# Edge phase of a graph layer: Q whole in f32, one f32 product per step for the queries, and gathers without waits for products

## The chip, the cores and the metric

The kernel runs on one core of a Trainium2 chip. The metric is the device time of one execution in microseconds. Engines: PE (TensorE, with PEld for its weight loads), DVE (VectorE), ACT (ScalarE), POOL (GpSimd, which here issues indirect DMAs) and SP (SyncE, which issues plain DMAs).

## The reference

One graph layer with attention over edges, then a mixture of experts. Only the first part matters here. N = 3125 nodes, 50000 edges sorted by destination, D = 256 = 4 heads x 64, 64 relations.

```python
enh = node_features + 0.1 * query_emb[None, :]
Q = (enh @ Wq + bq).reshape(N, H, D)
K = (enh @ Wk + bk).reshape(N, H, D)
V = (enh @ Wv + bv).reshape(N, H, D)
rel = rel_w[edge_relations]
mod_k = K[src] + 0.2 * rel[:, None, :]
scores = jnp.einsum('ehd,ehd->eh', Q[dst], mod_k) / D ** 0.5
seg_max = jax.ops.segment_max(scores, dst, num_segments=N)
ex = jnp.exp(scores - seg_max[dst])
denom = jax.ops.segment_sum(ex, dst, num_segments=N)
w = ex / denom[dst]
agg = jax.ops.segment_sum(w[:, :, None] * V[src], dst, num_segments=N)
```

What follows (output projection, layer norm, gate, top 2 of 16 experts) is the same in both kernels.

## The kernel before

**Tiling.** The nodes are 25 tiles of 128. The sorted edges are cut into 440 steps of up to 128 edges; two steps are a pair (220 pairs, numbered p), and all edges of a pair have destinations in one node tile. Four steps are a quad (110, numbered g), eight an octet (55, numbered o), 32 a chunk (14).

**Before the edges (to about 85 us).** The rows of x are normed, turned and multiplied into K and V, which go to a table in HBM (`kv_table`, 2 KB per node). Then Q is projected, tile by tile (`project_q`, L1659): five tiles before the first edges, the others beside pairs 0 to 14 (`q_tiles_at`). Q of each tile is kept as three bf16 pieces whose sum is the f32 value, in `q3`: ACT writes the first (`high_piece`, L1425), DVE the rest of it (`rest_of_q`, L743), ACT the second piece (`middle_piece`, L1429) and DVE the third (`low_piece`, L748).

**The edge phase (about 85 to 880 us).** Each engine has one order of work, written out by hand:

- POOL gathers K and V of the sources, four gathers per quad of 128 rows x 2 KB (`gather`, L626) into `ring`. The gathers of quad g wait until quad g - 4 is reduced (`a_red`), and two of them (u = 1, 2) also for the first and the second product of quad g - 3 (`a_prod`).
- SP loads, per octet, the destinations and types of the edges, spread over all partitions (`d_row`, `t_row`).
- DVE makes the 0/1 masks: `node_hot` (L857) compares the destinations with the partition number and writes `hot_t`, one mask of 128 x 1024 per octet, bf16; `type_hot` (L862) does it for the relations. Then, per octet: `add_relation` to K of two quads (L870), `multiply` by Q[dst] of four pairs (L877), `reduce` two quads to scores (L883), `add_sums` of four pairs, 26 pairs late (L889). Once per chunk come the running maxima (`maxima`, L896), and the factors by which sums are rescaled. `node_hot(o + 2)` is made in octet o between the fourth `multiply` and the second `reduce`.
- PE fetches Q[dst] with products of mask and Q (`queries`, L1724), three pairs ahead of `multiply` (AHEAD = 3), since three banks of PSUM take turns. It also makes the relations' rows (`relations`, L1736), turns the masks (`turn_hot`, L1744: eight transposes of the octet o - 4, in slot 2 of octet o, so behind `queries(4o + 5)` and the sums of that slot), and adds weighted V into per-node sums (`sums`, L1762, f32, 2 products per pair).
- ACT copies the turned masks (`take_hot`, L1492) and weighs V with the softmax weights (`weigh`, L1505).

A semaphore's `wait(eng, n)` lets the engine go on once event n has happened. `hot_t` has HB_N = 7 buffers: `node_hot(m)` waits until `turn_hot(m - HB_N)` is done, through `b_tr`. The mask of a quad is read by `queries`, by `turn_hot` and, one column, by a copy to `first`.

Of the kernel before, what the change touches and what calls it, by code (L numbers as in the profile page):

```python
# [5 lines left out]
F32 = mybir.dt.float32  # L6
BF16 = mybir.dt.bfloat16
# [49 lines left out]
HB_N = 7  # L57
# [87 lines left out]
def build(nc, A, out):  # L145
    ctx = ExitStack()
    with ctx:
# [89 lines left out]
        q3 = sb("q3", [P, NODE_TILES, 3 * D], BF16)  # L237
# [66 lines left out]
        q3_flat = q3[:, :, :].rearrange("p t c -> p (t c)").bitcast(F32)  # L304
        at[0] = 0
        x_again = carve(q3_flat, NT * D)
        xre = x_again.rearrange("p (t c) -> p t c", c=D)
        w_o = carve(q3_flat, KC * D).rearrange("p (k n) -> p k n", k=KC)
        gamma = carve(q3_flat, D)
        beta = carve(q3_flat, D)  # L310
        gate_w = carve(q3_flat, KC * NX).rearrange("p (k n) -> p k n", k=KC)
        gate_b = carve(q3_flat, NX)
        assert at[0] <= NODE_TILES * 3 * D // 2
# [14 lines left out]
        hot_t = eb("hot_t", [P, HB_N, 8 * P], BF16)  # L328
# [24 lines left out]
        at[0] = 3 * 4 * P  # L353
        hot_flat = hot_t[:, :, :].rearrange("p m c -> p (m c)").bitcast(F32)
# [3 lines left out]
        assert at[0] <= HB_N * 4 * P  # L358
# [13 lines left out]
        rest = carve(wv_flat, 3 * D).rearrange("p (s n) -> p s n", s=3)  # L372
# [86 lines left out]
        s_q, s_high, s_rest, s_mid, s_lo = (Count(sem(n)) for n in ("s_q", "s_high", "s_rest", "s_mid", "s_lo"))  # L459
# [116 lines left out]
        def _(pool):  # L576
# [49 lines left out]
            def gather(g):  # L626
                a_red.wait(pool, g - DEPTH)
                b_wv.wait(pool, 2 * (g + DEPTH - PLACES) + 1)
                for u in range(4):
                    if u in (1, 2):  # L630
                        a_prod.wait(pool, 2 * (g - DEPTH) + 1 + u if g >= DEPTH else -1)
                    pool.indirect_dma_start(ring[:, u, place(g) * D:(place(g) + 2) * D], None, kv_table,  # L632
                                            bass.IndirectOffsetOnAxis(ap=src_idx[:, 4 * g + u:4 * g + u + 1], axis=0)).then_inc(got[g % 4], 16)
# [75 lines left out]
        def _(v):  # L709
# [32 lines left out]

            def rest_of_q(t):  # L743
                s_high.wait(v, t)
                s_lo.wait(v, t - 3)
                v.tensor_tensor(rest[:, t % 3, :], q_bank(t), q3[:, t, 0:D], ALU.subtract).then_inc(s_rest.sem, 1)

            def low_piece(t):  # L748
                s_mid.wait(v, t)
                v.tensor_tensor(q3[:, t, 2 * D:3 * D], rest[:, t % 3, :], q3[:, t, D:2 * D], ALU.subtract).then_inc(s_lo.sem, 1)  # L750

            def pieces_of_q(first, end):
                for t in range(first, end):
                    rest_of_q(t)
                    if t >= 1:
                        low_piece(t - 1)

# [218 lines left out]
            def pieces_beside(p):  # L976
                for t in q_tiles_at(p - 2) if p > 1 else (Q_FIRST - 1,) if p else ():
                    low_piece(t)
                for t in q_tiles_at(p - 1) if p else ():
                    rest_of_q(t)  # L980

# [4 lines left out]
            pieces_of_q(0, Q_FIRST)  # L986
            for o in range(LAST_OCT):
# [18 lines left out]
                pieces_beside(4 * o + 1)  # L1006
# [8 lines left out]
                pieces_beside(4 * o + 2)  # L1015
# [3 lines left out]
                pieces_beside(4 * o + 3)  # L1019
# [368 lines left out]
        def _(act):  # L1388
# [83 lines left out]
            for i in range(NODE_TILES + 1):  # L1472
                if i < NODE_TILES:
                    high_piece(i)
                if i >= 1 and i != Q_FIRST:
                    middle_piece(i - 1)
                if i == Q_FIRST - 1:
                    middle_piece(i)
                    steps_links()
# [158 lines left out]
        def _(pe):  # L1638
# [20 lines left out]
            def project_q(t):  # L1659
                s_rest.wait(pe, t - 3)  # L1660
# [63 lines left out]
            def queries(p):  # L1724
# [50 lines left out]
            def turn_scores(ch):  # L1775
                if ch == 0:
                    s_rest.wait(pe, NODE_TILES - 1)
# [204 lines left out]
```

## Time and profile before

| | us |
|---|---|
| median of 3 runs | 1356.09 |
| lowest and highest | 1348.56, 1357.88 |
| profiled execution | 1346.19 |
| its span | 1344.4 |
| PE busy | 1080.3 (80%), 7032 matmul instructions |
| weight loads busy | 851.6 (63%) |
| DVE busy | 894.0 (66%) |
| ACT busy | 666.2 (50%) |
| POOL busy | 716.4 (53%) |
| mean granted TensorE clock | 0.868 of full |

The profile is of one execution, 10 us under the median of the runs. Busy time is the union of an engine's instructions; for PE the ends of matmuls are modelled, so that several in a row overlap. "Idle before" is time in which the engine did nothing ahead of an instruction of the group, with what seems to have ended it: "remote" is an event that the profile can't put down to an instruction of this core, "issue" means that it waited for nothing that the profile shows. An f32 product is two MATMUL instructions in the trace, a bf16 product one.

### The profile page before, as it was taken

To read this page: it belongs to the slowest core of one execution; us is meant where nothing else is said; L and a number is where in the kernel's file an instruction comes from. 1 tells how busy PE (TensorE), PEld (TensorE's weight loads), DVE (VectorE), ACT (ScalarE), POOL (GpSimd) and SP (SyncE) were. 2 spreads that over 40 slices of the span, in tenths; PEclk is the share of its full clock that TensorE was granted. 3 is DMA by queue.
4 is the path that set the end of the run, shared out by engine and by line. 5 is a ranking of instruction groups with operands and counts; after the bars stand their busy time and mean duration, and the time that the engine had idled before them with its cause. 6 is when DMAs were issued, how large, how long until landed. Compare 5 with 4: busy or idle time off the path is not lost.

```text
span 1344.4 us, 23897 instructions
## 1 busy us (share of the span) xinstructions
PE 1080.3 (80%) x7032; PEld 851.6 (63%) x7033; DVE 894.0 (66%) x1856; ACT 666.2 (50%) x2365; POOL 716.4 (53%) x714
## 2 busy tenths in 40 slices
PE   8978567776767777676677777799599999999997
PEld 3445345555545555555555565567389999999996
DVE  4767767677777877777777768889944444444443
ACT  5532356667667776576676766557511111111111
POOL 4455555555555655555556554756055555445663
PEclk9997777778888978777878878897699999999999
DMA  6266666656766666567666665602744444655332
GB/s 211 94 180 189 195 196 192 202 183 178 221 189 206 193 194 204 179 202 210 198 199 198 174 208 142 202 5 92 256 119 118 100 100 95 184 150 130 53 52 28
DMA packets 112993, 215.77 MB, mean 160 GB/s; under 512 B 19403, under 2 KB 57211, under 8 KB 112891
## 3 DMA queue, kind: packets, MB, share of 16 engines
q0 software_dynamic: 47488, 132.68, 36.7%
q1 hardware_dynamic: 59973, 80.16, 18.4%
q10 hardware_dynamic: 5430, 1.73, 0.6%
q8 instruction: 45, 0.74, 0.2%
q14 instruction: 57, 0.47, 0.1%
HBM read 191.96 MB, written 22.54 MB: 160 GB/s over the span
## 4 chain that ended last, share of the span: by engine, by line
PE 49%; DVE 21%; issue 16%; another core or an unknown queue 9%; ACT 2%; DMA 1%; DVEq 1%; SPq 0%; POOL 0%; POOLq 0%
PE qe_ps L1920 13%; PE bank L1929 8%; PE qe_ps L1732 6%; DVE ring L881 6%; PE bank L1772 5%; PE bank L1920 4%; DVE acc L893 3%; PE qe_ps L1772 2%; DVE ring L875 2%; DVE score L887 2%; PE qe_ps L1837 1%; PE qe_ps L1650 1%; PE qe_ps L1909 1%; PE bank L1650 1%
## 5 line engine op out<-in xcount | busy, mean ns | idle before, releaser
L632 POOL DMA_INDIRECT ring<-kv_table,src_idx x440 | 421.0, 957 | 330.4 <-DVE ring L881 181.5
L1502 ACT ACTIVATE wv<-ring,wgt 128x64 f32<-128x64 f32 x1628 | 407.3, 338 | 52.9 <-remote 46.5
L1732 PE MATMUL qe_ps<-q,hot_t 128*128 x1320 | 237.1, 316 | 140.0 <-issue 87.6
L1732 PEld LDWEIGHTS qe_ps<-q,hot_t 128*128 128x128 bf16 x1320 | 134.6, 110 | 209.0 <-issue 179.3
L1772 PE MATMUL bank<-wv,hotf 128*128 128x260 f32 x588 | 188.6, 451 | 25.2 <-issue 18.8
L697 POOL DMA_INDIRECT out<-room,slot_i x64 | 119.2, 1863 | 154.9 <-DMA out<-room,slot_i 81.4
L1920 PEld LDWEIGHTS qe_ps<-xg_t,ring 128*128 128x128 f32 x1536 | 181.4, 192 | 4.9 <-issue 1.7
L1621 ACT ACTIVATE act<-qe_ps 128x512 f32<-128x512 f32 x64 | 38.2, 597 | 294.7 <-PE bank L1920 140.9
L875 DVE TENSOR_TENSOR ring<-ring,bank 128x1024 f32<-128x1024 f32 x110 | 133.3, 1212 | 75.8 <-remote 63.3
L1920 PE MATMUL qe_ps<-xg_t,ring 128*128 128x128 f32 x1536 | 182.0, 275 | 1.3 <-issue 0.7
L881 DVE TENSOR_TENSOR ring<-ring,qe_ps 128x512 f32<-128x512 f32 x220 | 148.8, 677 | 26.1 <-remote 18.2
L1772 PEld LDWEIGHTS bank<-wv,hotf 128*128 128x128 f32 x588 | 122.8, 227 | 48.6 <-issue 21.3
L887 DVE TENSOR_REDUCE score<-ring 128x16 f32<-128x1024 f32 x110 | 133.3, 1211 | 0.2
L1496 ACT ACTIVATE hotf<-bank 128x512 f32<-128x512 bf16 x110 | 60.7, 593 | 142.8 <-remote 93.9
L1929 PE MATMUL bank<-ring 128*128 x512 | 121.0, 379 | 0.0
L1233 DVE COPY ring<-ring 128x2048 f32 x64 | 79.2, 1239 | 42.8 <-issue 37.3
L1929 PEld LDWEIGHTS bank<-ring 128*128 128x128 f32 x512 | 92.3, 190 | 10.1 <-issue 0.2
L1772 PE MATMUL qe_ps<-wv,hotf 128*128 128x260 f32 x292 | 92.3, 442 | 7.6 <-issue 4.6
L893 DVE TENSOR_TENSOR acc<-acc,bank 128x260 f32 x147 | 61.4, 417 | 52.9 <-remote 46.0
L691 POOL DMA_INDIRECT ring<-x_table,slot_i x64 | 71.1, 1111 | 34.1 <-issue 17.7
L1254 DVE TENSOR_TENSOR ring<-act,qe_ps 128x512 f32<-128x512 f32 x32 | 22.0, 687 | 78.8 <-ACT act L1621 71.3
L1772 PEld LDWEIGHTS qe_ps<-wv,hotf 128*128 128x128 f32 x292 | 60.3, 226 | 18.1 <-issue 5.4
(339 smaller groups left out, 1504.5 us busy)
## 6 DMA issues: line engine op xcount, KB each, us to landing
ring<-in_w SPq DMA_DIRECT2D x48, 512.0 KB, 7.1
t_row<-t_rows SPq DMA_DIRECT2D x55, 256.0 KB
d_row<-d_rows SPq DMA_DIRECT2D x55, 256.0 KB
ring<-kv_table,src_idx POOLq DMA_INDIRECT x440
kv_table<-ring SPq DMA_DIRECT2D x25, 256.0 KB, 2.0
out<-acc SPq DMA_DIRECT2D x26, 128.0 KB, 1.7
x_table<-ring SPq DMA_DIRECT2D x26, 128.0 KB, 1.9
ring<-in_x SPq DMA_DIRECT2D x12, 256.0 KB, 9.0
```

The lines of the kernel that those rows point to most:

```text
L632: pool.indirect_dma_start(ring[:, u, place(g) * D:(place(g) + 2) * D], None, kv_table, bass.IndirectOffsetOnAxis(ap=src_idx[:, 4 * g + u:4 ...
L697: pool.indirect_dma_start(out, bass.IndirectOffsetOnAxis(ap=slot_i[:, b:b + 1], axis=0), y_st[:, b % YB, :], None, compute_op=ALU.add).the ...
L875: v.tensor_tensor(k, k, rel_ps[:, at:at + 4 * HD].rearrange("p (u d) -> p u d", u=4).unsqueeze(2).to_broadcast([P, 4, H, HD]), ALU.add).th ...
L881: v.tensor_tensor(k, k, q_ps[p % AHEAD].rearrange("p (u c) -> p u c", u=2), ALU.mult).then_inc(a_prod.sem, 1)
L887: v.tensor_reduce(s, by_head(k_rows(g)), AX.X, ALU.add).then_inc(a_red.sem, 1)
L893: v.tensor_tensor(a, a, task_bank(("sum", pair))[:, 0:H * HB], ALU.add).then_inc(b_acc.sem, 1)
L1233: v.tensor_copy(w_block[:, b % 2, :], w[:, 0:2 * KC * HID]).then_inc(f_cw.sem, 1)
L1502: ins = act.activation(wv[:, g % WV_N, u, h, 0:HD], v_rows(g)[:, u, h * HD:(h + 1) * HD], ACT.Copy, scale=w[:, col:col + 1])
L1732: ins = pe.matmul(q_ps[p % AHEAD][:, u * D:(u + 1) * D], hot_t[:, p // 4 % HB_N, hot_cols(p, u)], tile_of(q3, q_tiles[p % 4])[:, k * D:(k ...
L1772: ins = pe.matmul(task_bank(("sum", p))[:, 0:H * HB], hotf[:, g % HF_N, u, :], wv[:, g % WV_N, u, :, :].rearrange("p h d -> p (h d)"), sta ...
L1920: ins = pe.matmul(bank[1 + 2 * m + i][:, h * P:(h + 1) * P], w_block[:, i, at:at + P], xg_t[:, i, c * P:(c + 1) * P], start=(c == 0), stop ...
L1929: ins = pe.matmul(bank[6 + i][:, 0:D], hid_t[:, i, c * P:(c + 1) * P], w[:, at:at + D], start=(c == 0), stop=(c == HC - 1))
```

## The change

- Q of each node tile is kept whole, in f32, in `q_all` (25 x 256 f32 per partition). ACT copies it from PSUM (`keep_q`); the three-piece form, `rest_of_q`, `low_piece`, `middle_piece`, `pieces_of_q` and `pieces_beside` go, with four of their semaphores. PE's `project_q` waits for that copy.
- `queries` makes one f32 product per step (mask times Q of the tile) where it made three bf16 products that add up.
- So the mask `hot_t` is f32. It takes 4 KB per buffer and partition instead of 2, and HB_N is 6 instead of 7. `turn_hot` reads it as bf16, every second element (the upper half of an f32 0 or 1 is the bf16 0 or 1). The copy to `first` comes an octet earlier, with the maxima.
- The four gathers of a quad no longer wait for products: only for the reduction of quad g - 4 and for the weighed V whose place they take.
- The weights of the later phases have a place of their own (`later`) where they shared that of `q3`.

```diff
-HB_N = 7
+HB_N = 6
-        q3 = sb("q3", [P, NODE_TILES, 3 * D], BF16)
+        q_all = sb("q_all", [P, NODE_TILES, D])
+        later = sb("later", [P, KC * D + 2 * D + KC * NX + NX])
...
-        hot_t = eb("hot_t", [P, HB_N, 8 * P], BF16)
+        hot_t = eb("hot_t", [P, HB_N, 8 * P])
...
                 for u in range(4):
-                    if u in (1, 2):
-                        a_prod.wait(pool, 2 * (g - DEPTH) + 1 + u if g >= DEPTH else -1)
                     pool.indirect_dma_start(ring[:, u, place(g) * D:(place(g) + 2) * D], None, kv_table,
...
-            def rest_of_q(t):
-                s_high.wait(v, t)
-                s_lo.wait(v, t - 3)
-                v.tensor_tensor(rest[:, t % 3, :], q_bank(t), q3[:, t, 0:D], ALU.subtract).then_inc(s_rest.sem, 1)
-
-            def low_piece(t):
-                s_mid.wait(v, t)
-                v.tensor_tensor(q3[:, t, 2 * D:3 * D], rest[:, t % 3, :], q3[:, t, D:2 * D], ALU.subtract).then_inc(s_lo.sem, 1)
...
-            pieces_of_q(0, Q_FIRST)
...
                     factor_rows(rows_due)
-                    v.tensor_copy(first[:, :], hot_t[:, rows_due * CS // 8 % HB_N, 0:1])
+                if maxima_due:
+                    v.tensor_copy(first[:, :], hot_t[:, maxima_due * CS // 8 % HB_N, 0:1])
                 if scored:
                     multiply(4 * o)
-                pieces_beside(4 * o)
...
-            def high_piece(t):
+            def keep_q(t):
                 s_q.wait(act, t)
-                act.activation(q3[:, t, 0:D], q_bank(t), ACT.Copy).then_inc(s_high.sem, 1)
-
-            def middle_piece(t):
-                s_rest.wait(act, t)
-                act.activation(q3[:, t, D:2 * D], rest[:, t % 3, :], ACT.Copy).then_inc(s_mid.sem, 1)
+                act.activation(q_all[:, t, :], q_bank(t), ACT.Copy).then_inc(s_qk.sem, 1)
...
             def project_q(t):
-                s_rest.wait(pe, t - 3)
+                s_qk.wait(pe, t - 3)
...
                 a_prod.wait(pe, p - AHEAD)
-                s_lo.wait(pe, min(p, NODE_TILES - 1))
+                s_qk.wait(pe, min(p, NODE_TILES - 1))
                 for u in range(2):
-                    for k in range(3):
-                        ins = pe.matmul(q_ps[p % AHEAD][:, u * D:(u + 1) * D], hot_t[:, p // 4 % HB_N, hot_cols(p, u)], tile_of(q3, q_tiles[p % 4])[:, k * D:(k + 1) * D],
-                                        start=(k == 0), stop=(k == 2))
+                    ins = pe.matmul(q_ps[p % AHEAD][:, u * D:(u + 1) * D], hot_t[:, p // 4 % HB_N, hot_cols(p, u)], tile_of(q_all, q_tiles[p % 4]), start=True, stop=True)
...
                 for u in range(8):
-                    ins = pe.transpose(turn_ps.bitcast(BF16)[:, u * P:(u + 1) * P], hot_t[:, o % HB_N, u * P:(u + 1) * P], identb[:, :])
+                    ins = pe.transpose(turn_ps.bitcast(BF16)[:, u * P:(u + 1) * P], hot_t[:, o % HB_N, u * P:(u + 1) * P].bitcast(BF16)[:, 1::2], identb[:, :])
```

## Rows read from the trace of the kernel before

**Rows 1.** Busy us (instructions) of each engine in two stretches, granted clock, DMA share

```profile
300.00:400.00 100.00, 70.62 (x491) 52.69 (x490) 75.44 (x140) 69.07 (x278) 57.16 (x61) 0.84 0.66 197
1000.00:1344.00 344.00, 335.61 (x2546) 322.34 (x2544) 151.27 (x305) 52.89 (x121) 176.70 (x118) 0.99 0.45 102
```

**Rows 2.** Groups by line: count | busy us, mean ns | idle us before, its releasers

```profile
L632 POOL DMA_INDIRECT ring<-kv_table,src_idx x440 | 421.0, 957 | 330.4 <-DVE ring L881 181.5 <-issue 98.9 <-DVE score L887 44.0
...
L881 DVE TENSOR_TENSOR ring<-ring,qe_ps 128x512 f32<-128x512 f32 x220 | 148.8, 677 | 26.1 <-remote 18.2 <-PE qe_ps L1732 7.6
...
L875 DVE TENSOR_TENSOR ring<-ring,bank 128x1024 f32<-128x1024 f32 x110 | 133.3, 1212 | 75.8 <-remote 63.3 <-DMA ring<-kv_table,src_idx 8.3 <-issue 4.2
L887 DVE TENSOR_REDUCE score<-ring 128x16 f32<-128x1024 f32 x110 | 133.3, 1211 | 0.2
...
L893 DVE TENSOR_TENSOR acc<-acc,bank 128x260 f32 x147 | 61.4, 417 | 52.9 <-remote 46.0 <-PE bank L1772 3.6 <-issue 1.6
...
L893 DVE TENSOR_TENSOR acc<-acc,qe_ps 128x260 f32 x73 | 30.4, 416 | 25.7 <-remote 22.5 <-PE bank L1772 2.2 <-PE qe_ps L1772 0.5
...
L860 DVE TENSOR_SCALAR hot_t<-d_row,part 128x1024 bf16<-128x1024 bf16 x55 | 26.6, 484 | 0.8 <-DMA d_row<-d_rows 0.7
...
L750 DVE TENSOR_TENSOR q<-wv,q 128x256 bf16<-128x256 f32 x25 | 10.1, 418 | 17.2 <-ACT q L1431 17.2
...
L827 DVE TENSOR_SCALAR acc<-hot_t 128x440 f32<-128x440 bf16 x1 | 0.4, 389 | 0.0
```

**Rows 3.** Timeline of POOL: start us, us, instruction, count [idle before, releaser]

```profile
167.96 0.94 POOL L632 DMA_INDIRECT ring<-kv_table,src_idx  x1 [2.26 <-DVE score L887]
...
602.73 0.94 POOL L632 DMA_INDIRECT ring<-kv_table,src_idx  x1 [2.85 <-DVE score L887]
...
614.26 0.95 POOL L632 DMA_INDIRECT ring<-kv_table,src_idx  x1 [0.30 <-issue]
...
656.07 0.94 POOL L632 DMA_INDIRECT ring<-kv_table,src_idx  x1 [2.86 <-DVE score L887]
...
820.11 0.94 POOL L632 DMA_INDIRECT ring<-kv_table,src_idx  x1 [2.85 <-DVE score L887]
```

**Rows 4.** Timeline of PE, ACT and DVE at the end of that burst

```profile
612.86 0.38 PE L1772 MATMUL qe_ps<-wv,hotf 128*128 128x260 f32 x1 [1.11 <-issue]
...
614.29 0.41 PE L1772 MATMUL qe_ps<-wv,hotf 128*128 128x260 f32 x1 [1.05 <-issue]
...
617.21 2.02 ACT L1502 ACTIVATE wv<-ring,wgt 128x64 f32<-128x64 f32 x8 [5.56 <-remote]
617.32 0.42 DVE L893 TENSOR_TENSOR acc<-acc,bank 128x260 f32 x1 [5.03 <-remote]
```

**Rows 5.** Timeline of one octet around its `node_hot` (L860), full clock

```profile
602.38 0.67 DVE L881 TENSOR_TENSOR ring<-ring,qe_ps 128x512 f32<-128x512 f32 x1
...
603.20 0.86 PE L1732 MATMUL qe_ps<-q,hot_t 128*128 x6 [0.54 <-DVE ring L881]
...
603.89 1.04 PE L1772 MATMUL qe_ps<-wv,hotf 128*128 128x260 f32 x4
603.91 0.48 DVE L860 TENSOR_SCALAR hot_t<-d_row,part 128x1024 bf16<-128x1024 bf16 x1
...
604.30 1.21 DVE L887 TENSOR_REDUCE score<-ring 128x16 f32<-128x1024 f32 x1
...
604.77 0.61 PE L1747 MATMUL bank<-identb,hot_t 128*128 128x128 bf16 x8
...
610.48 1.21 DVE L887 TENSOR_REDUCE score<-ring 128x16 f32<-128x1024 f32 x1
```

**Rows 6.** The same timeline after the burst, half clock

```profile
617.35 1.44 PE L1732 MATMUL qe_ps<-q,hot_t 128*128 x6
...
618.58 1.94 PE L1772 MATMUL bank<-wv,hotf 128*128 128x260 f32 x4
```

**Rows 7.** Timeline of POOL and DVE at a burst of seven

```profile
635.83 0.94 POOL L632 DMA_INDIRECT ring<-kv_table,src_idx  x1 [2.66 <-DVE ring L881]
...
645.84 1.22 DVE L875 TENSOR_TENSOR ring<-ring,bank 128x1024 f32<-128x1024 f32 x1 [3.37 <-remote]
```

**Rows 8.** DMA queue that loads instructions: packets, MB, share of 16 engines

```profile
q8 instruction: 45, 0.74, 0.2%
```

More of the change, by code:

```diff
@@ L301, in build @@
         assert at[0] <= NT * H * HB
-        q3_flat = q3[:, :, :].rearrange("p t c -> p (t c)").bitcast(F32)
+        x_again = q_all[:, :, :].rearrange("p t c -> p (t c)")
+        xre = q_all[:, :, :]
         at[0] = 0
[L306 to L313, printed above, removed]
+        w_o = carve(later, KC * D).rearrange("p (k n) -> p k n", k=KC)
+        gamma = carve(later, D)
+        beta = carve(later, D)
+        gate_w = carve(later, KC * NX).rearrange("p (k n) -> p k n", k=KC)
+        gate_b = carve(later, NX)
         w_expert = flat[:, 0:WB * WX].rearrange("p (b n) -> p b n", b=WB)
@@ L351, in build @@
         xn_st = late[:, 8 * P:8 * P + 2 * D].rearrange("p (b c) -> p b c", b=2)
-        at[0] = 3 * 4 * P
-        hot_flat = hot_t[:, :, :].rearrange("p m c -> p (m c)").bitcast(F32)
+        at[0] = 3 * 8 * P
+        hot_flat = hot_t[:, :, :].rearrange("p m c -> p (m c)")
         dval = carve(hot_flat, STEPS)
@@ L357, in build @@
         typ = carve(hot_flat, STEPS // 2, BF16)
-        assert at[0] <= HB_N * 4 * P
+        assert at[0] <= HB_N * 8 * P
         dst_t = late[0:PP, 0:4 * P].rearrange("p (q c) -> p q c", q=4)
@@ L371, in build @@
         w_q = [a[:, :, :].rearrange("p i c -> p (i c)") for a in (ends2, wgt)]
-        rest = carve(wv_flat, 3 * D).rearrange("p (s n) -> p s n", s=3)
         dif3 = carve(wv_flat, 3 * NT).rearrange("p (i t) -> p i t", i=3)
@@ L457, in build @@
         s_xn, s_xt, s_enh, s_mm, s_ev, s_kv = (Count(sem(n)) for n in ("s_xn", "s_xt", "s_enh", "s_mm", "s_ev", "s_kv"))
-        s_q, s_high, s_rest, s_mid, s_lo = (Count(sem(n)) for n in ("s_q", "s_high", "s_rest", "s_mid", "s_lo"))
+        s_q, s_qk = (Count(sem(n)) for n in ("s_q", "s_qk"))
         s_kst = [sem(f"s_kst{i}") for i in range(NS)]
@@ L741, in _ @@
                 row_scales(i)
-            def rest_of_q(t):
-                s_high.wait(v, t)
-                s_lo.wait(v, t - 3)
-                v.tensor_tensor(rest[:, t % 3, :], q_bank(t), q3[:, t, 0:D], ALU.subtract).then_inc(s_rest.sem, 1)
-            def low_piece(t):
-                s_mid.wait(v, t)
-                v.tensor_tensor(q3[:, t, 2 * D:3 * D], rest[:, t % 3, :], q3[:, t, D:2 * D], ALU.subtract).then_inc(s_lo.sem, 1)
[L752 to L756, printed above, removed]
             v.wait_ge(s_qe, 32)
@@ L973, in take_sums @@
                     average((p - EARLY_AT) // 2 - 1)
[L976 to L980, printed above, removed]
             tiles = []
@@ L1005, in _ @@
                     type_hot(1)
-                pieces_beside(4 * o + 1)
                 take_sums(o, 1)
@@ L1014, in _ @@
                     multiply(4 * o + 2)
-                pieces_beside(4 * o + 2)
                 take_sums(o, 2)
@@ L1018, in _ @@
                     multiply(4 * o + 3)
-                pieces_beside(4 * o + 3)
                 if o + 2 < BATCHES:
@@ L1470, in steps_links @@
                 ins.then_inc(event("diffs").sem, 1)
[L1472 to L1476, printed above, removed]
+            for i in range(NODE_TILES):
+                keep_q(i)
                 if i == Q_FIRST - 1:
-                    middle_piece(i)
                     steps_links()
@@ L1776, in turn_scores @@
                 if ch == 0:
-                    s_rest.wait(pe, NODE_TILES - 1)
+                    s_qk.wait(pe, NODE_TILES - 1)
                 bank_free(("score", ch))
```

## The prediction

> **What bounds the kernel now.** I read the busy time by stage first. Between 300 and 400 us no engine is full: DVE 75.4, PE 70.6, ACT 69.1 and POOL 57.2 of 100 us [rows 1]. From some 160 to 860 us the edge phase has this shape, octet after octet (an octet is 8 steps, 4 pairs, 2 quads; there are 55). From 1000 us to the end PE is full, and the change touches nothing there. So a gain or a loss is made in the edge phase, and each us per octet is worth some 50 us.
>
> The groups by line come second. DVE does per octet two `add_relation` (1.212), four `multiply` (0.677), two `reduce` (1.211), four `add_sums` (0.417) and two masks (0.48 each): 10.2 us with nothing else [rows 2]. Started back to back they overlap a little (0.42 of `add_sums` costs about 0.35), and the maxima of a chunk, once in four octets, bring it back to about 10.4. Beside these groups stands idle time put down to "remote": 63.3 + 46.0 + 22.5 + 18.2 = 150 us [rows 2]. DVE waits for hardly anything else: PE before `multiply` 7.6, a gather before `add_relation` 8.3.
>
> POOL's timeline shows the rhythm. The same burst comes back at 656.07 that began at 602.73: 53.34 us for four octets, 13.3 us each [rows 3]. Of these, 150 / 51 octets (160 to 860 us, at 13.3) = 2.9 us are the "remote" idle time and 10.4 are work. So within an octet DVE is the bound, and on top comes a disturbance.
>
> The timeline of the disturbance: POOL issued ten gathers back to back, 1.25 us apart, 602.73 to 614.26 [rows 3]. From 612 on, PE issues one instruction where it issued four: single f32 matmuls at 612.86 and 614.29 with over 1 us of "issue" before each. DVE sits idle 5.03 us to 617.32 and ACT 5.56 us, and all three go on together 3.06 us after the start of the last gather [rows 4]. I call this a crawl. POOL's timeline has 37 bursts of seven or more gathers, the first from 168.0 and the last from 820.1 us [rows 3]; each has such a stretch near its end, and no burst of up to four has one. Why it comes the trace does not say; that it goes with long bursts it does.
>
> **The change, part by part.**
>
> *1. The pieces of Q.* 25 `rest_of_q` and 25 `low_piece` leave DVE. The second kind is 25 at 418 ns with 17.2 us of waiting for ACT before it [rows 2]; 50 x 0.418 = 20.9 us of work, all before 165 us. ACT's middle pieces go too. There PE projects Q and POOL gathers (10.0 us per octet at 1.25), so an octet can't drop below about 11 from 13: four octets x 2 = 8, and 2 for the first products, which start sooner. Bounds 0 and 38 (20.9 + 17.2); I take -10.
>
> *2. One f32 product for three bf16.* Six bf16 matmuls of a pair hold PE from 603.20 until the next starts at 603.89: 0.69 us. Four f32 matmuls of `sums` (two products of 260 columns, two instructions each) hold it from 603.89 to 604.77: 0.88 us [rows 5]. With 256 columns that is 0.87, so each pair costs PE 0.18 us more, 0.7 per octet, 39 over 220 pairs. PE works 9.4 of 13.3 us per octet, products run three pairs ahead of `multiply`, and DVE waits 7.6 us in all for them: alone it costs nothing. Bounds 0 and 39; 0, except where it stands in part 4.
>
> *3. The node mask in f32.* `node_hot` writes 1024 f32 instead of bf16. Its 0.484 us is for bf16 to bf16; the nearest row with f32 out of bf16 in is 389 ns for 440 elements [rows 2]. Taking 0.16 us as fixed, as in (0.484 - 0.16) for 1024 bf16, leaves 0.229 us for 440, so 1024 take 0.53 + 0.16 = 0.69: +0.21 us on DVE, x 55 = +12. Bounds 0 and, if it went at the rate of `add_relation` (1.212 for 1024), +40.
> The Trainium skill speaks against this part too (VectorE: DVE Perf Modes, the perf-mode tier table and the cycle table of the errata): `tensor_scalar` falls from four elements per cycle to two where 4 bytes are written. Its estimate is (512 - 256) / 0.96 = 0.27 us each and +15 in the sum instead of +12; the row at 440 fits its two per cycle.
>
> *4. Six mask buffers for seven.* This is the main term. `node_hot(o + 2)` waits for `turn_hot` of m - HB_N. With 7 that is `turn_hot(o - 5)`, done an octet ago. With 6 it is `turn_hot(o - 4)`, which PE does in slot 2 of the same octet, behind `queries(4o + 5)` and `sums`, and `queries(4o + 5)` needs `multiply(4o + 2)`. The rows of one octet: `multiply(4o + 2)` ends at 603.05; PE queries at 603.20, sums at 603.89, turns at 604.77 to 605.38. DVE had started `node_hot` at 603.91 [rows 5]. It would now wait to 605.38, and to 605.56 with part 2: 1.65 us. Behind it in DVE's queue stand `reduce(2o + 1)`, which POOL's gathers wait for, and all of the next octet, so nothing hides it. At half clock PE took 1.23 us for the six query matmuls and 1.94 for four of `sums` [rows 6]; f32 queries and sums at 1.75 each (1.94 less the tail of the last), 1.1 for turning (0.61 at full clock), 0.15 to start, less the 0.86 that DVE needs anyway, are 3.9 us. The mean granted clock of 0.84 [rows 1] means half clock for a third of the time, much of it within the crawls, so I take 1.9 us. It holds for o = 4 to 52, 49 octets: +93. Bounds 81 and 191. A lower bound of nothing is excluded unless PE were already past slot 2, which its own wait for `multiply(4o + 2)` forbids.
>
> *5. The gathers.* The waits for `multiply` before u = 1 and u = 2 go, and 181.5 us of POOL's idle time stood with those products [rows 2]. That alone gives DVE nothing: POOL is ahead, and a gather holds DVE for 8.3 us in all. What changes is when gathers run. After each `reduce` four are free, 5.0 us of issuing. The second `reduce` of one octet starts at 604.30 and the first of the next at 610.48 [rows 5], 6.2 apart, so the two of one octet are about 4 apart (10.4 less 6.2), and 5.9 with part 4. So the eight of an octet go in one burst, with a gap of under 1 us in its middle, and then POOL pauses 1 to 2 us. Each octet has a burst long enough for a crawl. In the burst of ten DVE stopped 9.6 us after the start and went on 3.06 after the last gather's start; for eight that is 8.75 + 3.06 - 9.6 = 2.2 us. After the gather at 635.83 and a burst of seven from 637.89 DVE stopped at 642.47 (645.84 less 3.37), 6.6 us after the first [rows 7], which would give 8.75 + 3.06 - 6.7 = 5.1. Between these I take 2.6, near the first since POOL pauses before each burst: 2.6 - 2.9 = -0.3 per octet, x 50 = -17. Bounds -35 and +110.
>
> *6. Small.* `first` is copied an octet earlier (moved only). The late weights have a place of their own, but their loads still stand behind the last product. The transposes read every second bf16 of an f32; if their weight loads took as long as f32 ones it would lie under the matmuls before them. 0.
>
> Sum: -10 + 0 + 12 + 93 - 17 = +78. The profiled execution took 1346.2 us (span 1344.4), so 1424; the median of the three runs is 1356.1, 9.9 more, so **1434 us**.
>
> **The rivals.**
>
> *A. As summed.* 81 to 105 for part 4, -35 to +20 for part 5: 1400 to 1475. For it: a dependence that can be read off the timeline, on the engine that bounds the octet.
>
> *B. The crawls grow.* They begin after 6.7 us in each burst, as in [rows 7]: 5.1 - 2.9 = +2.2 x 50 = +110 instead of -17, 1434 + 127 = 1561 us; half of that 1500. For it: the bursts of seven. Against: those came within some us of the last crawl.
>
> *C. The crawls go* (the faster side). DVE needs 12.4 us for eight gathers instead of 10.4, so POOL is busy 10.0 of 12.4 us with a real pause, where in the stretches between crawls it had almost none. If a pause of 2 us after eight gathers is enough, the 150 us of "remote" go and the sum is -10 + 12 + 93 - 150 = -55: 1301 us. It decides for faster once the crawls fall below 1 us per octet. Against: bursts of seven crawl now.
>
> *D. The crawls are a throttle on what is issued per time.* Then an octet stays at 13.3 us as long as DVE's 12.4 fit in it; the crawls give up what part 4 takes and only the start gains: 1346 us, within 1%. The same comes out if the crawls are instruction loading: PE's queue loaded 45 blocks, 0.74 MB [rows 8], and an octet has 16 fewer PE instructions (6 x 2 x 4 = 48 of about 128 become 32), so 12% of 150 = 18 us less of it, which against part 4 leaves A at 1416.
> On this the Trainium skill (Runtime: NRT & Kernel Launch, Instruction fetch mechanics) says that instructions come in blocks of 16 KiB and that this is mostly hidden; the blocks agree with the row (0.74 MB / 45), and if hidden holds, the 18 us are none.
>
> **How the numbers follow.** A 0.45, B 0.17, C 0.20, D 0.18. The time is A's, 1434. The range reaches from just under C to the half-way case of B, 1295 to 1500; what is left out is most of B and the runs of C that also gain at the start. A's own range is 1400 to 1475. About 1% is what a measurement here can tell from no change: slower by over 1% are A and B, 0.62; faster C and a third of D, 0.25; within 1% the rest, 0.13.
>
> **What would show it.** Right: before `node_hot`, 1.5 to 2.2 us of DVE idle in nearly each octet from the fifth on, put down to PE's turning; `node_hot` at 0.69 us; four query matmuls per pair at 0.87 us warm; POOL in bursts of eight; 14.5 to 15 us per octet. Wrong: no idle time before `node_hot` (then part 4 fails and A with it); an octet at 13.3 with shorter crawls (D); no "remote" idle time (C); over 4 us of it per octet (B).

## The result, and the profile after

| | before | changed |
|---|---|---|
| median of 4 runs, us | 1353.90 | 1384.34 |
| lowest and highest | 1348.56, 1357.88 | 1378.26, 1386.36 |
| profiled execution, its span | 1346.19, 1344.4 | 1378.26, 1376.5 |
| mean granted clock | 0.868 | 0.892 |

The ratio is 1.022, with 1.0169 to 1.0271 as its 95% interval. The change makes the kernel slower, as forecast, but by 30 us and not by 78: 1384 us where 1434 was forecast. It lies inside the range, and under the bottom of A's own range of 1400 to 1475.

The groups by line of the changed kernel (count, then busy us and mean ns, then idle us before them and its releasers), to be held against [rows 2]:

```profile
L628 POOL DMA_INDIRECT ring<-kv_table,src_idx x440 | 429.8, 977 | 358.3 <-DVE score L867 224.9 <-issue 114.1 <-ACT wv L1464 11.1
...
L861 DVE TENSOR_TENSOR ring<-ring,qe_ps 128x512 f32<-128x512 f32 x220 | 149.2, 680 | 5.5 <-issue 3.5 <-remote 1.7
L855 DVE TENSOR_TENSOR ring<-ring,bank 128x1024 f32<-128x1024 f32 x110 | 133.5, 1214 | 32.2 <-remote 19.8 <-DMA ring<-kv_table,src_idx 12.2 <-PE bank L1701 0.2
...
L873 DVE TENSOR_TENSOR acc<-acc,bank 128x260 f32 x147 | 61.5, 418 | 5.6 <-PE bank L1732 2.2 <-remote 1.3 <-DVE acc L873 1.3
L840 DVE TENSOR_SCALAR hot_t<-d_row,part 128x1024 f32<-128x1024 bf16 x55 | 43.6, 795 | 189.5 <-PE bank L1707 110.9 <-remote 76.3 <-issue 1.8
...
L1693 PE MATMUL qe_ps<-q_all,hot_t 128*128 x880 | 287.3, 457 | 82.0 <-DVE ring L861 47.7 <-issue 33.3
```

Line 840 is `node_hot`, 855 `add_relation`, 861 `multiply`, 873 `add_sums`, 1707 the turning of the masks. Before, `node_hot` had 0.8 us of idle time ahead of it in all; now it has 189.5, and 110.9 of that is put down to the turning. The wait of part 4 is there. But the "remote" idle time, 150 us in the four groups of [rows 2], is now 76.3 + 19.8 + 1.7 + 1.3 = 99 us, and most of it has moved to the same place, ahead of `node_hot`. `node_hot` itself takes 0.795 us, not 0.69. `multiply` waits for PE as little as before.

The stretch from 300 to 400 us, the same columns as [rows 1]: DVE has fallen from 75.4 to 72.9 and POOL from 57.2 to 54.1.

```profile
300.00:400.00 100.00, 73.18 (x397) 56.09 (x395) 72.91 (x134) 65.40 (x260) 54.05 (x56) 0.85 0.60 184
```

Two octets of the timeline (start, length, engine, line). First one with the wait alone:

```profile
624.04 1.12 PE L1693 MATMUL qe_ps<-q_all,hot_t 128*128 x4 [0.47 <-DVE ring L861]
624.16 0.68 DVE L861 TENSOR_TENSOR ring<-ring,qe_ps 128x512 f32<-128x512 f32 x1
...
625.01 1.04 PE L1732 MATMUL qe_ps<-wv,hotf 128*128 128x260 f32 x4
...
625.88 0.61 PE L1707 MATMUL bank<-identb,hot_t 128*128 128x128 bf16 x8
...
626.61 0.93 DVE L840 TENSOR_SCALAR hot_t<-d_row,part 128x1024 f32<-128x1024 bf16 x1 [1.77 <-PE bank L1707]
```

DVE's fourth `multiply` ends at 624.84; PE does the queries, the sums and the turning; `node_hot` starts 0.73 after the turning began. The wait is 1.77 us, with PE at full clock (1.65 was worked out). Then one with a crawl in it:

```profile
606.57 0.68 DVE L861 TENSOR_TENSOR ring<-ring,qe_ps 128x512 f32<-128x512 f32 x1
...
608.75 0.61 PE L1707 MATMUL bank<-identb,hot_t 128*128 128x128 bf16 x8
...
609.76 0.95 POOL L628 DMA_INDIRECT ring<-kv_table,src_idx  x1 [0.30 <-issue]
611.77 1.09 ACT L1458 ACTIVATE hotf<-bank 128x512 f32<-128x512 bf16 x2 [4.69 <-remote]
611.84 0.75 DVE L840 TENSOR_SCALAR hot_t<-d_row,part 128x1024 f32<-128x1024 bf16 x1 [4.59 <-remote]
```

The masks are turned by 609.4, yet ACT and DVE, which both wait for that, go on together at 611.8, 2.0 us after the last gather of the burst was issued. Of the 4.59 us the wait would have taken about 2.2 by itself. So the crawl now lies partly over a time in which DVE waits anyway. The burst it follows has only four gathers (606.00 to 609.76), after a pause of 1.07 us: the prediction's "no burst of up to four has one", read from the kernel before, does not hold here.

Over the whole phase an octet grew from 13.66 to 14.41 us (from mask 9 to mask 54, the last: 206.7 to 821.28 us before, 209.01 to 857.53 after, 45 octets). The 13.3 of [rows 3] was one sample, a little low.

### The profile page after: what moved, and what is told of

The parts are those of the page before. It is cut to its first block, busy times and chain, and to the rows that moved or that the text cites. A ratio compares the mean times of both kernels' runs of the same rounds, so it can differ in the third digit from the quotient of the medians.

```text
span 1376.5 us, 22481 instructions
## 1 busy us (share of the span) xinstructions
PE 1114.7 (81%) x6592; PEld 897.1 (65%) x6593; DVE 893.8 (65%) x1806; ACT 663.0 (48%) x2340; POOL 729.0 (53%) x714
## 4 chain that ended last, share of the span: by engine, by line
PE 54%; DVE 22%; issue 12%; another core or an unknown queue 7%; DVEq 2%; ACT 1%; DMA 1%; POOL 0%; POOLq 0%; ACTq 0%; PEldq 0%
PE qe_ps L1880 12%; PE qe_ps L1693 9%; PE bank L1889 8%; PE bank L1732 5%; DVE ring L861 5%; DVE score L867 4%; PE bank L1880 4%; DVE ring L855 3%; PE qe_ps L1732 3%; DVE acc L873 2%; PE bank L1707 2%; PE qe_ps L1612 2%; PE bank L1701 2%; PE bank L1612 1%
## 5 line engine op out<-in xcount | busy, mean ns | idle before, releaser
L628 POOL DMA_INDIRECT ring<-kv_table,src_idx x440 | 429.8, 977 | 358.3 <-DVE score L867 224.9
L1693 PE MATMUL qe_ps<-q_all,hot_t 128*128 x880 | 287.3, 457 | 82.0 <-DVE ring L861 47.7
L1693 PEld LDWEIGHTS qe_ps<-q_all,hot_t 128*128 128x128 f32 x880 | 177.8, 223 | 129.0 <-issue 108.1
L1732 PE MATMUL bank<-wv,hotf 128*128 128x260 f32 x588 | 177.0, 434 | 45.4 <-DVE acc L873 45.4
L693 POOL DMA_INDIRECT out<-room,slot_i x64 | 119.6, 1869 | 152.4 <-DMA out<-room,slot_i 72.9
L1732 PEld LDWEIGHTS bank<-wv,hotf 128*128 128x128 f32 x588 | 125.1, 216 | 75.4 <-DVE acc L873 53.3
L840 DVE TENSOR_SCALAR hot_t<-d_row,part 128x1024 f32<-128x1024 bf16 x55 | 43.6, 795 | 189.5 <-PE bank L1707 110.9
L855 DVE TENSOR_TENSOR ring<-ring,bank 128x1024 f32<-128x1024 f32 x110 | 133.5, 1214 | 32.2 <-remote 19.8
L1732 PEld LDWEIGHTS qe_ps<-wv,hotf 128*128 128x128 f32 x292 | 63.9, 223 | 39.8 <-DVE acc L873 28.3
```

Of the source, the lines that this page charges most:

```text
L693: pool.indirect_dma_start(out, bass.IndirectOffsetOnAxis(ap=slot_i[:, b:b + 1], axis=0), y_st[:, b % YB, :], None, compute_op=ALU.add).the ...
L855: v.tensor_tensor(k, k, rel_ps[:, at:at + 4 * HD].rearrange("p (u d) -> p u d", u=4).unsqueeze(2).to_broadcast([P, 4, H, HD]), ALU.add).th ...
L1732: ins = pe.matmul(task_bank(("sum", p))[:, 0:H * HB], hotf[:, g % HF_N, u, :], wv[:, g % WV_N, u, :, :].rearrange("p h d -> p (h d)"), sta ...
```

## The experiments

**What differs between occasions.** The runs were made on six occasions after the first one. On five of them the same kernel before takes about 1166 us, on one about 1332, where it took 1354 at first. Every comparison below is against the kernel before on its own occasion. The difference is the crawls: where it takes 1166, DVE shows no "remote" idle time in any kernel. I call these occasions *calm* and the others (the first one and that of four runs) *crawling*. No edit of mine caused or removed that; what does is not known. It isn't the chip alone: the occasion of e5 (calm) and that of e6 to e9 (crawling) were on the same one.

| label | kernel | occasion | us | ratio (95%) |
|---|---|---|---|---|
| e1_six_masks | before, 6 mask buffers | calm | 1250.7 | 1.074 (1.068, 1.080) |
| e2_free_gathers | before, gathers without waits for products | calm | 1168.2 | 1.001 (0.998, 1.005) |
| e3_after_paced | changed, with these waits again | calm | 1287.9 | 1.105 (1.101, 1.109) |
| e4_turn_slot1 | changed, masks turned in slot 1 | calm | 1181.7 | 1.013 (1.008, 1.018) |
| e5_after_again | changed | calm | 1293.9 | 1.109 (1.107, 1.111) |
| e6_turn_slot0 | changed, turned in slot 0 | crawling | 1379.7 | 1.037 (1.029, 1.046) |
| e7_six_masks_2 | as e1 | crawling | 1412.9 | 1.063 (1.054, 1.072) |
| e8_turn_slot1_2 | as e4 | crawling | 1356.9 | 1.021 (1.012, 1.029) |
| e9_after_3 | changed | crawling | 1362.1 | 1.027 (1.018, 1.035) |
| e10_free_gathers_2 | as e2 | calm | 1167.1 | 1.001 (0.999, 1.004) |
| e11_after_paced_2 | as e3 | calm | 1289.1 | 1.106 (1.104, 1.109) |
| e12_six_free | before, 6 buffers and free gathers | calm | 1248.9 | 1.073 (1.069, 1.076) |
| e13_slot1_paced | as e4, with the waits again | calm | 1179.6 | 1.012 (1.010, 1.015) |
| e16_six_slot1 | as e1, turned in slot 1 | calm | 1176.0 | 1.008 (1.005, 1.011) |

**One part alone, on a calm occasion.** The theory was that the wait for a mask buffer costs the change its time and that the gathers are neutral; the rival, that the gathers' rhythm sets it.

```diff
-HB_N = 7
+HB_N = 6
                     factor_rows(rows_due)
-                    v.tensor_copy(first[:, :], hot_t[:, rows_due * CS // 8 % HB_N, 0:1])
+                if maxima_due:
+                    v.tensor_copy(first[:, :], hot_t[:, maxima_due * CS // 8 % HB_N, 0:1])
```

> The kernel before with six bf16 mask buffers for seven (and the copy to first an octet earlier), nothing else. In the changed kernel DVE stood 189.5 us before node_hot, but idle time put down to remote fell from 150 to 99 us. Theory 1 (the wait and the gathers are separate terms): this kernel pays the wait, 1.5 us x 49 octets = +73, and keeps its stalls of some 150 us: about 1427 us. Theory 2 (the stalls give up what the wait takes, whatever the gathers do): DVE idles some 70 us before node_hot, the other idle time falls by 30 to 50, and the time is 1380 to 1400 us. Theory 3 (a throttle on what is issued per time): 1354 us, no change.

```diff
-                    if u in (1, 2):
-                        a_prod.wait(pool, 2 * (g - DEPTH) + 1 + u if g >= DEPTH else -1)
```

> The kernel before without the two waits of the gathers for products, nothing else. Theory 1: the free gathers are what took 51 us of stalls away, and a wait of 7.6 us or less elsewhere, so this kernel is faster, 1300 to 1320 us. Theory 2 (the gathers matter little): 1345 to 1360 us. The rival of the prediction by which stalls grow with bursts of eight: 1400 us and more.

e3 puts those two lines back into the changed kernel:

> The changed kernel with the two waits of the gathers for products put back. Theory 1: the stalls come back, +50 us, about 1430 us. Theory 2: within 10 us of the changed kernel, 1375 to 1395 us. In both, idle time before node_hot stays.

e4 moves the turning one slot forward in the changed kernel, so that it stands a pair's products and sums earlier in PE's order and no longer behind `queries(4o + 5)`:

```diff
-TURN_SLOT = 2
+TURN_SLOT = 1
```

> The changed kernel with turn_hot one slot earlier on PE (slot 1 of the octet for slot 2), so that it stands behind queries(4o + 4) and needs multiply(4o + 1) only. If the wait of node_hot for turn_hot is a cost of its own (theory 1), DVE's idle time before node_hot put down to PE falls from 111 us to under 15 and the time by some 80: 1300 us, faster than both. By theory 2, where stalls come back as the wait goes: 1335 to 1355 us. By theory 3 (a throttle): no change, 1384 us.

Rows by line of e1 (`node_hot`), e2 (`node_hot`) and e4 (`node_hot`, then `add_relation`), one fence each:

```profile
L860 DVE TENSOR_SCALAR hot_t<-d_row,part 128x1024 bf16<-128x1024 bf16 x55 | 30.4, 552 | 90.7 <-PE bank L1748 89.9 <-DMA d_row<-d_rows 0.7
```

```profile
L858 DVE TENSOR_SCALAR hot_t<-d_row,part 128x1024 bf16<-128x1024 bf16 x55 | 26.5, 482 | 0.8 <-DMA d_row<-d_rows 0.7
```

```profile
L840 DVE TENSOR_SCALAR hot_t<-d_row,part 128x1024 f32<-128x1024 bf16 x55 | 42.9, 781 | 12.8 <-PE bank L1707 11.5 <-DMA d_row<-d_rows 0.6 <-issue 0.3
...
L855 DVE TENSOR_TENSOR ring<-ring,bank 128x1024 f32<-128x1024 f32 x110 | 133.2, 1211 | 22.3 <-DMA ring<-kv_table,src_idx 22.2
```

Six buffers alone cost 85 us, and 89.9 us of waiting for the turning stand ahead of `node_hot`: 1.83 us for each of 49 octets. (The forecast took 1.9 with the f32 product, 0.18 of it for that product.) Free gathers alone cost and gain nothing here; on a crawling occasion they were never run. Turned one slot earlier, the wait is nearly gone (11.5 us), and with it 112 of the 127 us that the change costs on a calm occasion (e5). On such an occasion DVE is full: e2 has it busy 98.36 of the 100 us from 300 on, which is why each us of wait there is a us of the end.

```profile
300.00:400.00 100.00, 79.06 (x627) 59.89 (x628) 98.36 (x189) 87.95 (x361) 75.58 (x79) 0.97 0.84 262
```

**The changed kernel on a calm occasion.** This was run because e3 stood at 1.105 where the changed kernel had stood at 1.022.

> The changed kernel itself. In the last runs the kernel before took 1165 us, not 1354, and no kernel of them had any idle time of DVE put down to remote: the stalls near the end of the gathers' bursts are absent there. If those stalls hid part of the wait before node_hot, then where they are absent the changed kernel costs its whole sum: the wait 121 us, the f32 mask 17, less 16 at the start, so 1165 + 122 = 1287 us (ratio 1.10), with gathers free or paced making no difference. Where the stalls are present again: 1384 us against 1354, as before. If instead free gathers cost something of their own where there are no stalls, it is over 1300 us.

Its `node_hot` and `add_relation` by line:

```profile
L840 DVE TENSOR_SCALAR hot_t<-d_row,part 128x1024 f32<-128x1024 bf16 x55 | 46.0, 838 | 123.2 <-PE bank L1707 122.5 <-DMA d_row<-d_rows 0.7
...
L855 DVE TENSOR_TENSOR ring<-ring,bank 128x1024 f32<-128x1024 f32 x110 | 133.1, 1210 | 19.1 <-DMA ring<-kv_table,src_idx 19.1
```

The wait is 122.5 us, not 89.9. The change costs 127 us here, and 30 where there are crawls. So the crawls cost the kernel before 1354 - 1166 = 188 us, and the changed kernel 1384 - 1294 = 90. The missing 100 us are there. The timeline shows why the wait grew by more than a product. After it stands the stretch from 567.60 to 570.80 us in the columns of [rows 1], with a granted clock of 0.50, between one at 1.00 before it and one at 1.00 behind it:

```profile
567.56 2.07 PE L1693 MATMUL qe_ps<-q_all,hot_t 128*128 x4 [2.02 <-DVE ring L861]
...
569.42 1.76 PE L1732 MATMUL bank<-wv,hotf 128*128 128x260 f32 x4
...
571.49 1.11 PE L1693 MATMUL qe_ps<-q_all,hot_t 128*128 x4
571.80 0.67 DVE L861 TENSOR_TENSOR ring<-ring,qe_ps 128x512 f32<-128x512 f32 x1
...
575.27 0.61 PE L1707 MATMUL bank<-identb,hot_t 128*128 128x128 bf16 x8
...
575.99 0.75 DVE L840 TENSOR_SCALAR hot_t<-d_row,part 128x1024 f32<-128x1024 bf16 x1 [3.51 <-PE bank L1707]
```

```profile
560.70:567.40 6.70, 3.21 (x20) 2.28 (x19) 4.93 (x9) 4.87 (x19) 4.91 (x5) 1.00 0.67 174
567.60:570.80 3.20, 3.20 (x8) 2.55 (x9) 3.20 (x5) 2.35 (x11) 1.89 (x2) 0.50 0.62 188
571.00:575.20 4.20, 4.20 (x35) 3.72 (x34) 1.48 (x3) 3.71 (x16) 3.06 (x4) 1.00 0.89 297
```

PE was busy for 3.21 of the 6.70 us up to 567.40 and idle for the last 2.02 us of them. It then does the octet's first f32 queries at half clock (2.07 us for four instructions, where the four at 571.49 took 1.11), falls behind, and turns the masks late: 3.51 us of waiting for 1.77. That is the rule in e5: of the 44 masks between 200 and 820 us 19 are waited for by over 3 us, and part of the 9 us before each of these was at a granted clock of 0.5 (11 of the other 25 have such a part too).

**The same edits on a crawling occasion.** Theory and rival were now whether crawls give up what a wait takes.

> The changed kernel with the masks turned in slot 0 of the octet, ahead of most of its products, so that node_hot finds its buffer free. Theory (wait behind the turning of the masks is what costs): on a chip without stretches of 'remote' idle time the idle time before node_hot is under 5 us in all, and the kernel stands within 1% of the kernel before: the longer mask (+17 us) against the pieces of Q left out (-8 to -16) and some 20 us of waiting for gathers in add_relation. Rival (f32 products hold PE too long by themselves): over 3% slower although the wait is gone. On a chip with such stretches: if they give up what the wait takes, the idle time total stays and the time is within 3% of the changed kernel's; if they are a cost of their own, it is 90 to 120 us faster than the changed kernel.

> The kernel before with six mask buffers for seven, nothing else. On a chip without 'remote' idle time: 1.07 times the kernel before, as on the first of them. On a chip with it, if these stretches give up what the wait takes: under 1.04 (under 50 us), with fewer us of remote idle time than the kernel before; if both are paid in full: 1.06 to 1.07 (85 us) and the remote idle time as before.

> The changed kernel with the masks turned in slot 1 for slot 2. On a chip without 'remote' idle time 1.01 to 1.02 times the kernel before. On a chip with it: if the stretches give up what the wait takes, the time is that of the changed kernel within 2%, the idle time moved from node_hot to remote; if not, it is 90 us or more faster.

> The changed kernel itself, for comparison on the same chip. 1.10 to 1.11 without 'remote' idle time in the kernel before, 1.02 with it.

`node_hot` in e7:

```profile
L860 DVE TENSOR_SCALAR hot_t<-d_row,part 128x1024 bf16<-128x1024 bf16 x55 | 26.7, 486 | 237.9 <-remote 215.0 <-PE bank L1748 22.1 <-DMA d_row<-d_rows 0.7
```

`node_hot` in e8:

```profile
L840 DVE TENSOR_SCALAR hot_t<-d_row,part 128x1024 f32<-128x1024 bf16 x55 | 41.4, 755 | 151.7 <-remote 133.6 <-PE bank L1707 17.3 <-DMA d_row<-d_rows 0.7
```

`add_sums` and `node_hot` in e6:

```profile
L873 DVE TENSOR_TENSOR acc<-acc,bank 128x260 f32 x147 | 61.7, 419 | 95.7 <-remote 93.2 <-DVE acc L873 1.3 <-PE bank L1732 0.8
L840 DVE TENSOR_SCALAR hot_t<-d_row,part 128x1024 f32<-128x1024 bf16 x55 | 41.8, 761 | 10.5 <-remote 10.2 <-DMA d_row<-d_rows 0.4
```

`node_hot` in e9:

```profile
L840 DVE TENSOR_SCALAR hot_t<-d_row,part 128x1024 f32<-128x1024 bf16 x55 | 44.0, 801 | 171.6 <-PE bank L1707 138.5 <-remote 22.5 <-issue 10.1
```

What crawls cost each kernel (crawling less calm): before 165 us (188 on the first occasion), six buffers alone 1413 - 1251 = 162, changed with slot 1 1357 - 1182 = 175, changed 1362 - 1294 = 68 (90 on the first). Two things follow. Six buffers alone pay for both, wait and crawls in full: a wait by itself absorbs nothing, which contradicts rival D as it was written. But in the changed kernel something of the kind does hold: taking the wait away (e8) gains 5 us, which is within the noise, where it gained 112 on a calm occasion, since 133.6 us of "remote" idle time take its place, and with slot 0 (e6) the crawls move on to `add_sums` (93.2 and 40.2 us), `add_relation` (39.0) and `multiply` (20.2), and the kernel is 18 us slower than the changed one. So it matters where the crawl falls relative to the wait. Five rows of the timeline of e7:

```profile
434.92 0.61 PE L1748 MATMUL bank<-identb,hot_t 128*128 128x128 bf16 x8
...
435.74 0.95 POOL L632 DMA_INDIRECT ring<-kv_table,src_idx  x1 [0.30 <-issue]
...
436.56 0.27 PE L1733 MATMUL qe_ps<-q,hot_t 128*128 x1 [0.92 <-issue]
...
437.27 0.27 PE L1733 MATMUL qe_ps<-q,hot_t 128*128 x1 [0.44 <-issue]
...
438.42 0.49 DVE L860 TENSOR_SCALAR hot_t<-d_row,part 128x1024 bf16<-128x1024 bf16 x1 [5.73 <-remote]
```

and the same place in e9:

```profile
477.20 2.07 PE L1693 MATMUL qe_ps<-q_all,hot_t 128*128 x4 [1.07 <-DVE ring L861]
...
484.61 0.95 POOL L628 DMA_INDIRECT ring<-kv_table,src_idx  x1 [0.30 <-issue]
484.66 0.61 PE L1707 MATMUL bank<-identb,hot_t 128*128 128x128 bf16 x8
...
486.73 1.08 ACT L1458 ACTIVATE hotf<-bank 128x512 f32<-128x512 bf16 x2 [3.76 <-PE bank L1707]
486.80 0.75 DVE L840 TENSOR_SCALAR hot_t<-d_row,part 128x1024 f32<-128x1024 bf16 x1 [4.69 <-PE bank L1707]
```

In e7 the last gather is issued 0.8 us after the turning begins and the crawl holds DVE for 2.8 us more than the 0.7 that it needs from there. In e9 the octet is one of those with PE at half clock: the wait would have been 3.1 to 3.5 us, as in e5, the last gather goes out with the turning, and from the turning on DVE loses 1.4 us beside its 0.7. Counted over the octets between 200 and 820 us, by the idle time ahead of `node_hot`:

| kernel | idle over 3.3 us | their mean | mean of the others | last gather against start of turning, median of all | start of turning to `node_hot`, median of all |
|---|---|---|---|---|---|
| e1, calm | 2 of 44 | 3.88 | 1.69 | | 0.72 |
| e7, crawling | 31 of 41 | 5.99 | 1.69 | 1.32 after | 3.96 |
| e5, calm | 15 of 44 | 4.00 | 1.81 | | 0.72 |
| e9, crawling | 24 of 44 | 4.69 | 1.94 | 0.12 after | 1.22 |

In the changed kernel fewer octets are hit, and 15 long waits are there without any crawl, where six buffers alone have 2.

Mask by mask (9 to 52) the two effects come apart. For the 18 masks that e5 waits for by over 3 us, the mean wait goes from 3.78 us (e5) to 4.78 (e9): crawls add 1.0 us where the wait is long already. With six buffers alone the same masks go from 2.30 (e1) to 6.11 (e7), +3.8. For the other 26 masks the changed kernel goes from 1.60 to 2.51, and 20 of them stay under 3.3 us; six buffers alone go from 1.52 to 4.08. So overlap with a long wait can account for about half of what is saved (18 x 2.8 = 50 us). The other half (26 x 1.65 = 43 us) is in octets with a short wait, most of which show no crawl there at all, and overlap does not explain that.

Per octet (mask 9 to mask 54), on a calm and on a crawling occasion; e2 stands in for the kernel before, of which there is no calm trace:

| kernel | calm | crawling | difference |
|---|---|---|---|
| before | 10.32 (e2) | 13.66 | 3.3 |
| six buffers alone | 12.17 (e1) | 15.10 (e7) | 2.9 |
| changed, slot 1 | 10.80 (e4) | 14.04 (e8) | 3.2 |
| changed | 13.17 (e5) | 14.07 (e9), 14.41 (first) | 0.9, 1.2 |

**Which part does it.** The candidates: the free gathers (G), the f32 product (F), or only both with the wait (W). e10 to e13 were to tell them apart, and needed a crawling occasion:

> The kernel before without POOL's waits for products, nothing else. Where the kernel before shows 'remote' idle time of DVE (about 1330 to 1356 us): theory G (the gathers' new rhythm is what shortens these stretches): 60 to 100 us faster than the kernel before, remote idle time under 90 us. Theory F (the f32 products are, with 16 PE instructions fewer per octet): within 2% of it. Theory W (they give up what a wait takes, so only together with the wait before node_hot): within 2% of it. Without such idle time in the kernel before: within 0.5% of it, as on the first such occasion.

> The changed kernel with the waits for products put back. Where the kernel before shows remote idle time: G says that they grow back, 1430 to 1460 us or 1.07 to 1.09 times the kernel before; F and W say the time of the changed kernel within 2%, 1.01 to 1.04. Without such idle time: 1.105.

> The kernel before with six mask buffers and without POOL's waits for products; bf16 products and mask stay. Where the kernel before shows remote idle time: G and W say under 1.03 (six buffers alone: 1.063); F says 1.06. Without such idle time: 1.07 to 1.075, as six buffers alone.

> The changed kernel with the masks turned in slot 1 and the waits for products put back: f32 product and f32 mask with nearly no wait before node_hot. Where the kernel before shows remote idle time: F says below the kernel before, 0.96 to 0.99; G and W say 1.02 or more. Without such idle time: 1.00 to 1.01, since the waiting for gathers in add_relation (22 us against 15) would be as it was.

All four fell on a calm one, and so did two further tries of e12 (e14_six_free_2 1.070, e18_six_free_3 1.074) and of e3 (e15_after_paced_3 1.102, e17_after_paced_4 1.105):

> The kernel before with six mask buffers and without POOL's waits for products, once more, for an occasion on which the kernel before shows remote idle time. There theory G (free gathers shorten it) and W (so does any wait together with them) say under 1.03 times the kernel before, where six buffers alone made 1.063; theory F (the f32 products do it) says 1.06. Without remote idle time 1.07 to 1.075 again.

> The changed kernel with the waits for products put back, once more. With remote idle time in the kernel before: G says 1.07 to 1.09 times it, F says 1.01 to 1.04 as the changed kernel. Without it 1.105 again.

> The changed kernel with the waits for products put back. With remote idle time in the kernel before: G (free gathers shorten it) says 1.07 to 1.09 times it, F (the f32 products do) 1.01 to 1.04. Without it 1.105.

> The kernel before with six mask buffers and free gathers. With remote idle time in the kernel before: G says under 1.03, F says 1.06. Without it 1.07.

So G, F and W stay open. What these runs do show: free gathers are neutral with six buffers as well (1.073 for 1.074), and the changed kernel with the waits put back stands at 1.102 to 1.106, where e5 stood at 1.109. They also show that long bursts don't make a crawl by themselves: in e2 POOL issued up to 41 gathers less than 1.45 us apart, and DVE has no "remote" idle time. The last run prices the wait at its cheapest, without f32 product and mask:

> The kernel before with six mask buffers and the masks turned in slot 1: bf16 products, bf16 mask, gathers as before. It prices the wait alone at its cheapest: without remote idle time the idle time before node_hot is under 12 us (11.5 with f32 products) and the kernel stands within 1% of the kernel before, which puts the 1.2% that remain with f32 product and mask together down to these. With remote idle time: theory W (only together with the wait in slot 2 do the stretches shrink) says within 2% of the kernel before.

1.008: slot 1 gets back 75 of the 85 us of six buffers. The f32 product and mask, less the pieces of Q, then cost 1179.6 - 1176.0 = 4 us on top (e13); with slot 2 they cost 1289 - 1250 = 39. Most of the 35 us between is the half-clock octets of e5: 15 x (4.00 - 1.81) = 33 us.

## Why the prediction was wrong in size and right in direction

**Part 4, the buffer wait (+93): right in place and cause, 29 us too small.** It is 1.77 us where PE has its full clock, and 89.9 us over the phase with bf16 products. With the f32 products it is 122.5 us (2.5 us per octet for the 1.9 forecast), inside the bounds of 81 to 191. The 0.18 us per octet that I added for them was too little, because only one pair's product was counted: in 19 octets of e5 products ran at half clock before the turning and PE didn't catch up.

**Part 5, the crawls (-17): this is the step that failed.** They went from 188 to 90 us, -98, far outside the bounds of -35 to +110. The failed step is the sentence that took 2.6 us of crawl per octet as a sum beside the wait; the runs showed 0.9 (e9) to 1.2 (first occasion). I had priced the crawl by its distance from the gathers, and DVE's wait by PE's timeline, and added them without asking whether they fall on the same time. Both end ahead of `node_hot`. The distance from the last gather held roughly: where there is a crawl, DVE goes on some 2.0 to 2.7 us after the last gather's start, for 3.06 in [rows 4]. (The "remote" time by line, 150 and then 99 us, under-reads the fall: ahead of `node_hot` it holds part of the wait too.) But in the changed kernel that gather goes out as the masks are being turned, while DVE waits already. By the masks above, overlap accounts for about half of the 98 us; why the other octets escape, and which part of the change brings it about, stays open. A second premise failed too: that each burst of eight is long enough for a crawl. On calm occasions much longer bursts had none. The gathers themselves, the other half of part 5, gave DVE nothing on calm occasions, as said (1.001); on a crawling one that is not shown.

**Part 1, the pieces of Q (-10):** on calm occasions the third mask comes 19.9 us after the first two (82.81 to 102.72 in e5) and 27.1 with the pieces (82.81 to 109.90 in e2). -7, and in e4, where hardly a wait follows, still -7 four octets on. On the first, crawling occasion this gain didn't last: the third mask came at 100.18 us for 115.23, but then DVE stood 14.85 us in one crawl, behind 24 gathers back to back (the first crawl of the kernel before is at 178 us), and the fourth came at 126.10 for 128.08.

```profile
112.07 0.95 POOL L628 DMA_INDIRECT ring<-kv_table,src_idx  x1 [0.30 <-issue]
...
116.89 1.22 DVE L855 TENSOR_TENSOR ring<-ring,bank 128x1024 f32<-128x1024 f32 x1 [14.85 <-remote]
```

**Part 2 (0):** by itself nothing, as forecast; `multiply` waits 0.3 us in e5. Its cost is in part 4.

**Part 3 (+12):** 55 x (0.795 - 0.484) = +17. The row of 440 elements under-read it. The Trainium skill's estimate (VectorE: DVE Perf Modes, the perf-mode tier table), +15, came nearer. By that page the mask grows by 0.27 us; here it grew by 0.31.

**The sum by what was measured:** -7 + 17 + 122 - 98 = +34, for +30. The forecast was -10 + 12 + 93 - 17. Only the first three are measured by themselves, and on calm occasions, where they make 132 for 127; the -98 is the difference between the two kinds of occasion, so that the whole sum comes out near +30 is no test of it.

**The rivals.** D, with 0.18, came somewhat nearer in time (1346 us, 38 off, for A's 1434, 50 off): in the changed kernel the crawls gave up 98 us while the wait took 122. Its mechanism is not borne out: e7 shows that there is no general throttle, since six buffers alone pay both, and an octet did not stay at 13.3 us but went to 14.41. A's own range should have read 1404 to 1483 by its terms. D's variant by instruction loading is not supported either: the instruction queue loaded the same in e5 and in e9 (packets, MB), and only e9 crawls.

```profile
q8 instruction: 40, 0.66, 0.2%
```

In the trace of the kernel before, only 3 of DVE's 40 "remote" stops of over 1 us have the start of a packet of that queue in them.

B did not happen: an octet's bursts are of four and eight now, and crawls cost less. Nor did C: 99 us of "remote" idle time are left.

## What to carry to other kernels

Two stalls that may end at the same instruction are not simply two terms of a sum: put each on the timeline, see which ends last, and price what stands out behind the other. Nor may you take it that one hides the other: in e7 both ended ahead of `node_hot` and both were paid in full. Taking a buffer away changes which instance a wait is for; work out from both engines' orders whether that one is done an octet ago or only behind the next products, and move the releasing instruction forward in the same edit (one slot got back 112 of 127 us here, on calm occasions). Run the kernel before again beside each experiment: here its own time moved by 188 us, six times what the change did.

## What was unexpected

The crawls are not a property of the kernel alone. The kernel before takes 1166 us without them and 1332 to 1354 with them, within 1.4% on one occasion; the changed kernel 1294 and 1362 to 1384. Each of the two kernels ran on occasions of both kinds, and only the "remote" idle time tells these apart. At the end of a crawl the engines that wait go on within 0.2 us of each other ([rows 4]; ACT 611.77 and DVE 611.84 after). While it lasts PE often issues single instructions ([rows 4], and e7 at 436.56 and 437.27). The cause isn't known, and nothing in the kernel was found to switch it on or off.

The half clock returns within an octet: after a stretch in which PE was busy for 3.21 of 6.70 us, the last 2.02 idle, the granted clock was 0.50 and the next four f32 instructions took 2.07 us for 1.11 (e5, 567.56 and 571.49). The pause alone does not tell: in the kernel before, PE went on at full clock after 2.08 us of idle time (608.30). The half clock cost more than the product's own extra time, 33 us for 0.18 x 49 = 9.

No kernel tried here beats the kernel before. Free gathers alone stand level with it (1.001); the best with six buffers, e16, is 0.8% slower.
